# The inverse of 32x32 triangular blocks by two rounds of squares, and a new step order, in a gated delta rule

## The reference

```python
def step(S, inp):
    qt, kt, vt, at, bt = inp
    err = jnp.einsum('bhvk,bhk->bhv', S, kt) - vt
    S = at[..., None, None] * S - bt[..., None, None] * err[..., None] * kt[:, :, None, :]
    o = jnp.einsum('bhvk,bhk->bhv', S, qt)
    return (S, o)
...
o = _gated_delta(q, k, v, alpha, beta, scale)
mu = o.mean(-1, keepdims=True)
var = ((o - mu) ** 2).mean(-1, keepdims=True)
o = (o - mu) * jax.lax.rsqrt(var + 1e-05) * ln_w + ln_b
g = jax.nn.sigmoid(x @ Wg).reshape(B, T, H, DV)
o = (o * g).reshape(B, T, H * DV)
return o @ Wo
```

## Time and profile before

| what | value |
|---|---|
| median of 3 runs | 2126.78 us (2126.25 to 2129.01) |
| the profiled execution | 2118.2 us, its span 2116.5 us |
| mean granted TensorE clock over the span | 0.951 |
| PE busy over the span | 1928.3 us (91%) |
| DVE, ACT, POOL busy over the span | 1567.2, 1333.5, 743.7 us |

### The profile page before, as it was taken

One profiled execution on the slowest core, in us unless ns is written; L12 is line 12 of the kernel. 1 busy time (PEld: TensorE's weight loads), 2 busy tenths in 40 slices (PEclk: granted clock), 3 DMA queues, 4 the chain that ended last, 5 costly groups with the idle time before them and its releaser, 6 DMA issues. The chain is left out here.

```text
span 2116.5 us, 68799 instructions
## 1 busy us (share of the span) xinstructions
PE 1928.3 (91%) x29180; PEld 1458.4 (69%) x29180; DVE 1567.2 (74%) x3017; ACT 1333.5 (63%) x2887; POOL 743.7 (35%) x1037
## 2 busy tenths in 40 slices
PE   7589999996885699999999999999999999999767
PEld 4233333333774578888888888888888888888656
DVE  2699999971754578788888877778788788887356
ACT  1248888884431357677766667667666677676443
POOL 2423444451322223333333333333333333332233
PEclk8779999998996799999999999999999999999879
DMA  3301212101000101011011011011011011010011
GB/s 122 89 21 43 53 31 64 46 18 39 1 1 9 62 12 55 23 42 48 23 49 41 23 44 45 23 37 53 23 35 55 23 40 50 23 34 26 1 43 41
DMA packets 74336, 79.86 MB, mean 38 GB/s; under 512 B 13424, under 2 KB 60912, under 8 KB 74032
## 3 DMA queue, kind: packets, MB, share of 16 engines
q1 hardware_dynamic: 74032, 75.46, 12.3%
HBM read 66.13 MB, written 8.91 MB: 35 GB/s over the span
## 5 line engine op out<-in xcount | busy, mean ns | idle before, releaser
L1711 DVE SCALAR_TENSOR_TENSOR d_acc<-ps,d_par,d_acc 128x1023 f32<-128x1023 f32 (+2 forms) x288 | 365.1, 1268 | 29.5 <-ACT d_acc L1590 28.5
L1403 PE MATMUL ps<-x1p,d_wh 128*128 128x512 f32 x1024 | 358.5, 432 | 16.6 <-DVE d_acc L1711 9.8
L514 ACT ACTIVATE a_prob<-ps 128x512 f32<-128x512 f32 (+2 forms) x640 | 311.3, 560 | 87.3 <-PE ps L483 83.1
L537 DVE TENSOR_REDUCE a_mx<-ps 128x2 f32<-128x1024 f32 (+2 forms) x320 | 336.6, 1111 | 33.5 <-PE ps L467 20.3
L1337 POOL TENSOR_TENSOR d_og_l<-d_o_g,d_og_h 128x512 fp32r<-128x512 f32 x64 | 82.0, 1281 | 426.0 <-ACT d_og_h L1687 426.0
L1403 PE MATMUL ps<-x1p,d_wl 128*128 128x512 f32 x512 | 204.4, 399 | 0.0
L1403 PEld LDWEIGHTS ps<-x1p,d_wh 128*128 128x128 f32 x1024 | 170.8, 194 | 40.1 <-DVE d_acc L1711 10.6
L1590 ACT ACTIVATE d_acc<-ps,d_par 128x512 f32<-128x512 f32 x192 | 149.0, 776 | 72.3 <-PE ps L1403 71.3
L462 PE MATMUL ps<-k,q 48*128 48x512 bf16 (+3 forms) x768 | 142.6, 348 | 34.5 <-DMA k<-scratch_k 20.3
L483 PE MATMUL ps<-q,k 51*128 51x512 bf16 (+2 forms) x640 | 161.4, 364 | 5.6 <-ACT a_prob L514 3.1
L497 PE MATMUL ps<-a_prob,a_v 128*32 128x512 f32 (+3 forms) x1536 | 164.4, 501 | 0.2
(11 more groups left out here) (244 smaller groups left out, 4793.8 us busy)
## 6 DMA issues: line engine op xcount, KB each, us to landing
d_abc<-scratch_alpha SPq DMA_DIRECT2D x32, 512.0 KB, 5.1
d_gb<-scratch_g SPq DMA_DIRECT2D x32, 512.0 KB, 4.0
d_wr<-in_dw SPq DMA_DIRECT2D x16, 512.0 KB, 4.9
scratch_q<-p_parts SPq DMA_DIRECT2D x24, 128.0 KB, 2.4
q<-scratch_q SPq DMA_DIRECT2D x32, 96.0 KB
scratch_y<-a_oT SPq DMA_DIRECT2D x64, 36.0 KB
x_tok<-in_x SPq DMA_DIRECT2D x2, 1024.0 KB
q<-scratch_q SPq DMA_DIRECT2D x32, 64.0 KB
```

The lines of the kernel that those rows point to most:

```text
L514: inc(nc.scalar.activation(prob[:, y % PB, g:g + heads, off:], ps[:, PLACE["st", n, x], 0:heads * w].rearrange("p (h c) -> p h c", c=w), A ...
L537: inc(nc.vector.tensor_reduce(out, ps[:, bank:bank + 2, 0:heads * w].rearrange("p r (h c) -> p r h c", c=w), AX.X, ALU.max, negate=True), ...
L1403: last = nc.tensor.matmul(ps[:, bank, :], wp[g][:, k, i, :], x(part), start=(k == 0 and j == 0), stop=(k == KE - 1 and j == 2))
L1711: inc(nc.vector.scalar_tensor_tensor(acc[i][:, d:T], taps[:, 0:T - d], par[p][:, 4 * i + j:4 * i + j + 1], acc[i][:, d:T], ALU.mult, ALU.a ...
```

## The change

The 8x8 blocks are inverted as before. The two levels of `y` and `z` are replaced by a second round of `sq`, `qd`, `oc`: with T the inverse of the 8x8 diagonal blocks and B minus the rest of the 32x32 block, the matrix N = T B has zero fourth power, because there are four blocks, so that the inverse is (I+N)(I+N^2)T. One round takes `sq.1` (N), `qd.1` (N^2 and T + N T together) and `oc.1`. POOL makes both masked parts in one operation (`above`), DVE transposes both in one (`below`). The arrays `am` and `y2` go, `y2` becomes a view of `above`. One constant is loaded instead of two. The order lists are new on every engine, and part E is now used. The core of the diff:

```diff
-LEVELS = (8, 16)
...
-        "c_low": np.stack(low, 1).astype(np.float32),
-        "c_first": -first.astype(np.float32),
+        "c_minus": np.stack(minus, 1),
...
+        O.gate.1.1 S.qd.1.0 O.ks.5 O.pw.4 S.qd.1.1 S.v_turn.0 O.w.5 X.o_turn.1 S.oc.1.0 S.oc.1.1 O.qs.5 O.pw.5 O.s.5 L.proj.1.0.0 L.proj.1.0.1
...
-        y2 = sb("y2", [P, TB, 64])
+        y2 = above[:].rearrange("p i c t -> p (i c t)").rearrange("p (c t) -> p c t", t=64)
...
-            for dst, name in ((low, "c_low"), (first, "c_first"), (eye, "c_eye"), (ln, "ln")):
+            for dst, name in ((minus, "c_minus"), (eye, "c_eye"), (ln, "ln")):
...
-                inc(nc.gpsimd.tensor_tensor(ttp[:], ad[:], each(first[:]), ALU.mult), "mt")
-                levels = [P, len(LEVELS), TB, QB]
-                inc(nc.gpsimd.tensor_tensor(am[:], ad[:].unsqueeze(1).to_broadcast(levels), low[:].unsqueeze(2).to_broadcast(levels), ALU.mult), "am")
+                both = [P, 2, TB, QB]
+                inc(nc.gpsimd.tensor_tensor(above[:], ad[:].unsqueeze(1).to_broadcast(both), minus[:].unsqueeze(2).to_broadcast(both), ALU.mult), "above")
...
-            def squares(n, h):
-                W("m", n, 1)
-                inc(packed(h, lambda c, r: ttp[r, c, :], tp), "sq")
+            def squares(n, i, h):
+                if i == 0:
+                    W("below", n, 1)
+                    inc(packed(h, lambda c, r: above[r, 0, c, :], below[:, 0]), "sq")
+                else:
+                    W("ttp", n, h + 1)
+                    inc(packed(h, lambda c, r: ttp[r, c, :], below[:, 1]), "sq")
...
-            def y(n, l, h):
-                if l == 0 and h == 0:
-                    W("am", n, 1)
-                W("tp", n, 2 * l + h + 1)
-                inc(packed(h, lambda c, r: am[r, l, c, :], tp), "y")
-
-            def z(n, l, h):
-                W("ttp", n, 2 * l + h + 1)
-                W("ym", n, 2 * l + h + 1)
-                inc(packed(h, lambda c, r: ttp[r, c, :], ym), "z")
...
             def first_(n):
-                W("mt", n, 1)
-                inc(nc.vector.transpose(tp[:].rearrange("p c t -> p (c t)"), ttp[:].rearrange("p c t -> p (c t)")), "m")
+                W("above", n, 1)
+                inc(nc.vector.transpose(below[:].rearrange("p i c t -> p (i c t)"), above[:].rearrange("p i c t -> p (i c t)")), "below")
...
+                whole = sq[:, 1] if i == 0 else tp
+                inc(nc.vector.tensor_tensor(whole[:, half(h)], tp[:, half(h)], half_of(h), ALU.add), "tp")
```

More of the change, by code:

```diff
@@ L674, in delta_inputs @@
     r, c = np.arange(P)[:, None] % QB, np.arange(QB)[None, :]
-    low = [((c // n) % 2 == 1) & (r // n == c // n - 1) for n in LEVELS]
-    first = (r // SMALL == c // SMALL) & (c > r)
+    small = r // SMALL == c // SMALL
+    minus = [-(small & (c > r)).astype(np.float32), -(~small & (c > r)).astype(np.float32)]
     return {
@@ L1138 @@
     "PE": """
[L1139 to L1142, removed]
@@ L1145 @@
+        S.gate.0.0 S.qs.1 S.s.1 S.gate.0.1 S.pw.1 S.ks.2 X.out.1 X.out.2 S.qs.2 S.w.2 L.sq.0.0 L.sq.0.1 S.s.2 S.pw.2 E.proj.0.0.0 E.proj.0.0.1
+        L.qd.0.0 E.proj.0.1.0 S.ks.3 L.qd.0.1 L.oc.0.0 S.w.3 X.out.3 E.proj.0.1.1 S.qs.3 S.s.3 S.pw.3 L.oc.0.1 L.sq.1.0 S.ks.4 S.gate.1.0 O.o_turn.0
+        S.w.4 S.qs.4 L.sq.1.1 S.s.4""",
     "ACT": """
-        X.w.6 S.tap.1.1 O.z64 O.v_turn.1 X.pw.6 X.w.7 O.y128 S.silu.0 X.pw.7 O.z128 S.silu.1 O.w.0 S.tap.2.0 O.pw.0 X.norm.0 S.tap.2.1 O.w.1
-        S.blocks O.gate.0 O.pw.1 O.gate.1 O.w.2 S.sq.0 S.sq.1 X.norm.1 O.pw.2 X.o_turn.0 O.w.3 L.tap.0.0 S.silu.2 O.pw.3 L.tap.0.1 S.y.0.0 S.y.0.1
@@ L1148 @@
-        O.w.4 X.og.0 O.pw.4 X.o_turn.1 S.v_turn.0 S.y.1.0 S.y.1.1 O.w.5 X.og.1 S.diag S.y64 O.pw.5 L.tap.1.0""",
+        O.z64 O.v_turn.1 X.pw.6 X.w.7 O.y128 S.silu.0 X.pw.7 O.z128 S.silu.1 S.tap.2.0 O.w.0 S.tap.2.1 O.pw.0 O.w.1 S.blocks O.gate.0 O.pw.1 O.w.2
+        S.sq.0.0 S.sq.0.1 X.norm.0 X.norm.1 O.pw.2 L.tap.0.0 O.w.3 L.tap.0.1 S.silu.2 O.pw.3 S.sq.1.0 O.w.4 S.sq.1.1 X.o_turn.0 O.gate.1 S.v_turn.0
+        O.pw.4 O.w.5 X.o_turn.1 X.og.0 O.pw.5 S.diag L.tap.1.0 O.w.6 S.y64 L.tap.1.1 X.og.1""",
@@ L1149 @@
     "DVE": """
[L1150 to L1153 removed]
+        X.o_turn.0 S.oc.1.0 S.oc.1.1 O.s.5 O.ks.6 X.o_turn.1 O.pw.2 S.k_turn.0 O.pw.3 O.pw.4 O.s.6 L.conv.1.0 O.ks.7 O.pw.5 L.conv.1.1 L.conv.1.2
@@ L1154 @@
+        S.k_turn.1 O.pw.6 X.out.0 O.pw.7 L.decay S.s.0 L.pair.0 L.pair.1 S.ks.1 O.stats L.pair.2 L.pair.3 L.conv.2.0 S.s.1 L.conv.2.1 S.ks.2 L.first
+        L.conv.2.2 L.sq.0.0 X.out.1 S.s.2 L.sq.0.1 S.pw.0 L.qd.0.0 S.pw.1 S.ks.3 X.out.2 L.qd.0.1 L.oc.0.0 X.out.3 S.s.3 E.conv.0.0 S.ks.4 L.oc.0.1
+        L.sq.1.0 E.conv.0.1 S.s.4 L.sq.1.1 E.conv.0.2 S.ks.5 L.qd.1.0 L.qd.1.1""",
     "POOL": """
-        O.qg X.wo S.blocks S.one X.og.0 X.og.1 L.split L.scalars O.stats""",
+        X.wo X.stats S.blocks S.one L.split X.og.0 S.qg X.og.1 L.scalars""",
@@ L1690, in _ @@
             act.wait_ge(c_made, 9)
-            E_.walk("ACT", {"tap": tap, "gate": gate_, "silu": silu, "v_turn": v_turn, "blocks": blocks, "sq": squares, "y": y, "y64": y64, "y128": y128, "diag": diag, "z64": z64, "z128": z128,
+            E_.walk("ACT", {"tap": tap, "gate": gate_, "silu": silu, "v_turn": v_turn, "blocks": blocks, "sq": squares, "y64": y64, "y128": y128, "diag": diag, "z64": z64, "z128": z128,
                             "w": w_, "pw": pw, "norm": norm, "o_turn": o_turn, "og": og})
```

104 lines of the change are left out of this document (45 added, 59 removed).

## The result

The changed kernel took 2106.74 us (median of 4 runs, 2104.37 to 2107.03), the kernel before 2127.82 beside it: a ratio of 0.9902, 95% interval 0.9886 to 0.9918, so 21 us or 1.0% faster. In the profiled executions it is 2104.37 against 2118.2, 13.8 us less; that execution of the kernel before is an earlier one and not among its four runs here.

A forecast was written before the change was run, and what follows sets the result against it. PE's own issue was taken as the bound, 39.4 us a unit. Terms -4.3 - 1.5 - 0.4 - 1.0 + 2.0 = -5.2 us took the median from 2126.8 to 2121.6 us, range 2111 to 2136.

The forecast's parts named there:

- the middle stretch: Scans from 1220 to 1621 us, 0.65 us a unit above the floor; fewer PE instructions save 1.5 us (0 to 7).
- rival D: Breaks in PE's small groups vanish, 7 us of excess goes, 2110 to 2116 us; chance 0.14.
- the ends: Before the first scan and after the last, serial chains set the time; -1 us at the end, bounds -5 and +8.
- PE's issue: PE's steps one after another set a unit's time; fewer small products gain 0.14 us a unit, 4.3 us (3 to 8).
- The waits for DVE: PE waits at the first squares and at `ks.2`; 0.07 us a unit, 2 us in all (0 to 15).
- Start: First products wait for the last small constant; one fewer DMA issued ahead saves 0.4 us.
- The difference carried from the profiled execution to the median: Median of runs stood 8.6 us above the profiled execution; the same was added to 2113.0, giving 2121.6.
- B: DVE makes PE wait at `ks.2` and first `sq`, up to 0.5 us a unit; some 2132 us, slower; chance 0.22.
- C: The first and last stages grow as a unit's steps stretch over more stages; 19 us, 2136 to 2141; chance 0.09.
- E: On PE `qd` groups cost no more than `sq`; 12 us less, about 2109 us; chance 0.05.

The follow-up runs named there:

- new_math_old_order: The changed kernel with the step lists of the kernel before, its new steps put where the old ones stood; 2104.48 us, ratio 0.9912.

## Why the prediction was off

**The step that failed is the term for the middle stretch.** The prediction put it as "If PE's supply of instructions is behind it, the change helps", and took a fifth of the excess, 1.5 us, with 7 as the upper bound. The runs show that supply is behind it, and that 12.9 - 0.5 = 12.4 us of breaks in small groups go, in a sum of 13.8; with those outside the groups (1.9 us beyond the usual distance of rows) and the one at 1961.87 it is 15.1. Two things made it too small. The row was read as one odd event, though counting PE's rows in the same trace would have put 14 of 15 breaks on one row in 256; with that, rival D would have had more than its 0.14. And the excess was taken from the middle scans only. The breaks of the first stages (2.42 us at 733.69, 0.38, 1.42 and 0.37 up to 809.25) were inside "the ends", where I had a serial chain that couldn't change: the first three intervals fell by 4.7 us, and those four breaks are 4.6. That the one is the other is not shown: new_math_old_order has none of the four either, and its first three intervals fell by only 1.7 us.

**The other terms**, in the profiled executions:

- PE's issue, -0.14 us a unit: right in size, as far as the runs tell. In the lists of before the floor fell from 39.32 to 39.19, and in the changed kernel with the divided mask it is 39.18 on the mean behind the first three intervals. The pairs and the lone `qd` came as said: in the timeline after, a pair of `sq` or `oc` halves takes 0.68 us (1439.09 to 1439.77) and a lone `qd` 0.58 (1436.04 to 1436.62), where 0.55 was forecast.

```profile
1436.04 0.65 PE L1473 MATMUL ps<-d_sq,d_ym 32*32 32x64 f32 x32
1436.62 0.49 PE L1513 MATMUL ps<-d_state,d_kq 128*128 128x128 f32 x2
...
1439.09 0.75 PE L1452 MATMUL ps<-d_tp,d_ym 32*32 32x32 f32 x64
1439.77 0.49 PE L1520 MATMUL ps<-d_state,d_kq 128*128 128x128 f32 x2
```

- The waits for DVE, +0.07 us a unit: the mechanism was right and one of its two places was the one named, the first `sq` behind the longer mask and transpose. The size was 0.29 us, measured by taking it away: behind the first three intervals the mean is 1105.2/28 = 39.47 us with one mask and 1097.2/28 = 39.18 with two halves. `first` on 512 columns takes 712 ns, where 680 was assumed. The other place named, `s.1` to `ks.2`, shows no wait; the second wait is at `ks.7`, where the prediction had counted slack.

```profile
L1728 DVE STREAM_TRANSPOSE d_below<-d_above x27: 711/712/712, 870.4 to 1896.9; 128x512 f32<-128x512 f32 x27
...
  POOL d_above L1352: 9.4, 27
```

- The two together: of the breaks before, 4.6 us lie in the first three intervals, 8.7 in the 28 later ones (7.36 in small groups, 1.36 outside) and the rest behind the last scan, where that of the changed kernel lies too. Less their breaks the later intervals are (1110.8 - 8.7)/28 = 39.36 us before and 39.47 after, +3.0 us in all where -2.3 was forecast. So the saving of the mathematics on PE's time was eaten by the wait that it made, and DVE's 175 of 200 us (167 forecast) belongs to that.
- Start: -0.7 us (-0.4 forecast). From the last scan to the last product: 2002.97 - 1926.0 = 77.0 us in place of 79.7, -2.7; breaks are 1.8 of that (0.95, 0.6 and 0.81 before, 0.54 after), and 0.9 is left, close to the 1.0 forecast.

```profile
2002.97 0.41 PE L1561 MATMUL ps<-d_wo_h,d_og_l 128*128 128x256 f32 x1
```

The sum is -15.1 + 3.0 - 0.7 - 0.9 - 0.1 (what is left of the first three intervals) = -13.8 us, that of the profiled executions.

**The difference carried from the profiled execution to the median, 8.6 us, failed too.** Of the kernel before it was 9.6 us in the runs beside the changed one, and of the changed kernel 2.4. That accounts for the other 7 us of the 21. The kernel before spreads from 2114.4 to 2135.9 us over four further jobs, with medians of 2120.7 to 2127.7, and the changed kernel, whose eight runs there go from 2101.9 to 2114.8, stands 15.0 us below it in the last of them. That before's undisturbed median holds more or longer breaks than its profiled execution would explain this, but breaks are seen only in profiled executions: it is argued and not shown.

**The rivals.** D came true, with twice its price. B's mechanism did as well, at 0.29 us a unit in place of 0.5. That is above the 0.23 from which it was to decide; that the kernel is faster all the same is D's doing. C did not: the first intervals after are 38.4 to 38.8 us. E is refuted: the lone `qd` takes 0.58 us. A lone `sq` half takes 0.38 us in the same stretch, from its start to the next step's. The Trainium skill's page "TensorEngine Tiling (Array Packing)", section Performance Considerations, holds that each matmul carries an overhead of about 60 cycles, by which the two would be nearly alike; the 0.58 and 0.38 us disagree.

**What stays open:** why some packets begin late. The 512 KB loads are not what most breaks need: of the 17 at borders before, 15 had no packet of the data queue in the 6 us ahead of them. Open too is what sets the longer of the two intervals that take turns.
